# A gated linear-attention block with an NVFP4 feed-forward: two VectorE dequantising instructions of weight chunk 0 moved behind the first attention step's projections and output rows

## The chip, the cores and the metric

The kernel runs on one NeuronCore of one Trainium2 chip. The metric is the device time of one execution in microseconds (us). Core 0 is the only core, so its time is the time of the kernel.

## What is computed

Two residual layers on x of shape 4 x 512 x 512, in float32, each behind a layer norm. The reference, cut to what matters here:

```python
x = x + attn(layernorm(x))      # DIM 512, 4 heads of 128, chunks of 128 tokens
x = x + ffn(layernorm(x))       # MLP_DIM 4096

# attn, per batch row b, head h and chunk n of 128 tokens
q, k, v = x @ Wq + bq, x @ Wk + bk, x @ Wv + bv
k = k / max(norm(k), 1e-12)
alpha, beta = sigmoid(x @ Walpha + balpha), softplus(x @ Wbeta + bbeta)
cla = cumsum(log(alpha + 1e-6))                 # inside the chunk
decay = where(causal, exp(cla - cla.T), 0)
attn = (q @ k.T) * beta.T * decay
y_local = attn @ v
delta = v.T @ (k * beta * exp(cla_end - cla))
y = (q @ state.T) * exp(cla) + y_local
state = state * exp(cla_end) + delta

# ffn: W from two 4-bit codes per byte and one scale per 32 values
gate, up = xt @ Wg.T, xt @ Wu.T
out = (gelu(gate) * up) @ Wd.T
```

## The kernel before, in words

The 2048 tokens are 16 tiles of 128 (`NT = 16`), held in SBUF as `X1`. Every float32 matrix operand of the large products is split into a float16 high part and a float16 low part (what the high part leaves), and three products of parts replace one of float32. The program is written out by hand, engine by engine: TensorE (PE), ScalarE (ACT), VectorE (DVE), GpSimd (POOL) and the SyncE queue (SP) each have their own fixed list of instructions, and semaphores tie the lists together. Nothing is scheduled by a planner, so what stands on an engine's list behind a waiting instruction waits too.

The order of the work is: layer norm and transposes of the 16 tiles with the early q, k, v projections; the gates; then 16 attention steps T = 0 to 15, each one chunk of one batch row; then the feed-forward, whose parts begin inside the attention steps. The change is at the border of attention steps 0 and 1.

What each engine does in a step T, in the order of its list:

- **PE**: `head(T)` transposes the chunk's keys into a PSUM bank, "kn" (L414), and multiplies q by k (L423). Then come the step's fills, which are projections of the next batch rows (L348, twelve matmuls each): in step 0 the keys (1,1) and (1,2), with the decay matrix of step 1 between them; in step 1 the queries (1,2) and the values (1,0). Then `mid(T)`: the state's increment from the weighed keys (L434), the local output from the weighed attention (L440) and, from step 1 on, the global output (L447). In `mid(1)` L434 waits for `weigh_keys(1)` and L440 waits for `weigh(1)`, both on DVE. The PSUM banks are taken in a ring of five (`Banks([0, 1, 5, 6, 7])`); a bank is waited for until the engine that reads it has released it. The bank of "kn" of step 1 is the one that the projection of keys (1,1) filled, so L414 of step 1 waits until DVE has moved that projection to SBUF (L959).
- **ACT**: `norms_of_k(T)` squares and sums the transposed keys (L710), then the exponential of the next step's decay (L700), the fills of kind q (L671), a copy of transposed tokens (L660, from step 1), and, in the steps of `DEQUANTED`, the high part of both halves of a weight chunk (L748). So ACT's list has L748 of chunk 0 ahead of the four L710 of step 1.
- **POOL**: `head(T)` turns the sums into the keys' scales: maximum (L1325), power (L1327), two products (L1329, L1330), then scales the decay (L1333). After that come the mask of the next step (L1316), the decay rows (L1310) and, in the steps of `DEQUANTED`, the low part of both halves of the chunk (L1359). So POOL's list has L1359 of chunk 0 ahead of `head(1)`.
- **DVE**: `weigh_keys(T)` (L1013) needs POOL's L1329; `weigh(T)` (L1023) needs POOL's L1333; the norm of the second layer for the tile before (L932, from step 1); the fills of kinds k (L959) and v (L954); `mid(T)`, which is the state (L1033 or L1040), the output row (L1045, L1052) and the statistics of the new row (L921, L923); the low part of the transposed tokens (L938, from step 1).

A weight chunk k is dequantised in parts. DVE makes the float16 bit patterns from the codes in `dq_bits(k)` (four instructions: L1087, L1093, L1098, L1101) and the float32 weights from bits and scales in `dq_finish(k)` (L1122, one for each of two halves, into the one buffer `wf`). ACT then casts each half to its high part (L748) and POOL subtracts for the low part (L1359). SP may load the chunk after next only when `dq_finish(k)` is done (L1504, L1507).

`DEQUANTED` says in which steps this happens:

```python
DEQUANTED = (0, 1, 4, 5, 8, 9)
```

Chunks 0 to 5 are finished in these steps, and `dq_bits` of each stands at the end of the step before (chunk 0's ahead of step 0). Steps 0 and 1 finish chunks 0 and 1; steps 4 and 5 finish chunks 2 and 3 in the same way.

Of the kernel before, what the change touches and what calls it, by code (L numbers as in the profile page):

```python
# [59 lines left out]
def fills(T):  # L60

    b, c = T // 4, T % 4
    out = [QKV_FIRST[c]] if b == 0 else []
    if b in (1, 2):
        out += [(kind, b + 1, h) for kind, h in KQ[2 * c:2 * c + 2]]
    if T == 0:
        out.insert(0, ("k", 1, 1))
    elif T + 3 < NT:
        out.append(("v", (T + 3) // 4, (T + 3) % 4))
    return out  # L70


DEQUANTED = (0, 1, 4, 5, 8, 9)
# [42 lines left out]
def wlo_count(k, nib):  # L116

    if k < 6:
        return 2 * k + nib + 1
    g, c = k // 6 - 1, k % 6  # L120
    return 12 + 6 * g + {0: 1, 2: 2, 4: 3 + nib, 5: 5 + nib}[c]


def pair_count(k):

    return 2 * (k // 6 - 1) + k % 6 // 2 + 1


def block_kernel(nc, x, wqkv, bqk, bv, wab, bab, codes, scales, out, cla):
    with ExitStack() as ctx:  # L130
# [82 lines left out]
        def h4(ap):  # L213
            return ap.rearrange("p (h t) -> p h t", h=4)
# [24 lines left out]
        def place(k):  # L239
            return k % 2 if k < 10 else 0  # L240
# [7 lines left out]
        def codes_in(k):  # L248

            return tb[:, :] if k < 6 else PS[7 if k < 10 else 5][:, :].bitcast(I32)  # L250
# [661 lines left out]
        def _(eng):  # L912
# [12 lines left out]
            def apply(tag, T):  # L925
                s = T % 2
                dv.wait_ge(s_rstd[tag], 2 * T + 2)
                if T >= 2:
                    dv.wait_ge(s_turn[tag], T - 1)
                elif tag == "n2":  # L930
                    dv.wait_ge(s_turn["n1"], NT - 1 + T)
                eng.tensor_scalar(xh[:, s, :], X1[:, T, :], mv[:, s, 0:1], rs[:, s, 1:2], ALU.subtract,  # L932
                                  ALU.mult).then_inc(s_xh[tag], 1)

            def turn_low(tag, T):
                hi, lo = (XT[:, a, :, 128 * T:128 * T + 128] for a in range(2))
                dv.wait_ge(s_hi[tag], T + 1)
                eng.tensor_tensor(lo, h4(PS[bank_of[tag, T]][:, :]), hi, ALU.subtract).then_inc(s_lo[tag], 1)  # L938
# [8 lines left out]
            def project(kind, b, h):  # L947
                f, done = 1.0 / (XS * QS), 4 * b + h + 1
                if kind == "v":
                    dv.wait_ge(s_const, 64)  # L950
                    dv.wait_ge(s_mm["v"], done)
                    if b >= 1:
                        dv.wait_ge(s_yl, done - 4)
                    eng.scalar_tensor_tensor(vv[:, h, :], PS[bank_of["v", b, h]][:, :], f, bvb[:, :], ALU.mult,  # L954
                                             ALU.add).then_inc(s_qkv["v"], 1)
                elif kind == "k" and b >= 1:
                    dv.wait_ge(s_const, 64)
                    dv.wait_ge(s_mm["k"], done)
                    eng.tensor_scalar(kT[:, b % 2, h, :], PS[bank_of["k", b, h]][:, :], f, bqk_s[:, 4 + h:5 + h],  # L959
                                      ALU.mult, ALU.add).then_inc(s_qkv["k"], 1)  # L960
# [44 lines left out]
            def weigh_keys(T):  # L1005
                b, c, s = T // 4, T % 4, T % 2
                if c < 3:
                    dv.wait_ge(s_kn, T + 1)
                    dv.wait_ge(s_kscale, 4 * T + 3)
                    dv.wait_ge(s_ss, T + 1)  # L1010
                    if T >= 1:
                        dv.wait_ge(s_dl, 3 * b + c)
                    eng.tensor_tensor(h4(kwb[:, :]), h4(PS[bank_of["kn", T]][:, :]),  # L1013
                                      kn_s[:, s, 4, :].unsqueeze(2).broadcast_to([128, 4, 128]),
                                      ALU.mult).then_inc(s_kw, 1)

            def weigh(T):
                s = T % 2
                dv.wait_ge(s_S, T + 1)
                dv.wait_ge(s_decw, T + 1)  # L1020
                if T >= 1:
                    dv.wait_ge(s_yl, T)
                eng.tensor_tensor(att[:, :], PS[4][:, :], dec[:, s, :], ALU.mult).then_inc(s_attn, 1)  # L1023
# [45 lines left out]
            def act_tile(i):  # L1069
                dv.wait_ge(s_gu["up"], i + 1)  # L1070
                inter(i, pair(i)[1][:, :], i + 1)
                inter_low(i)

            def gather(n, tt):
                T = 4 * (n % 4) + tt
                dv.wait_ge(s_dn, 4 * n + tt + 1)
                eng.scalar_tensor_tensor(X1[:, T, :], PS[bank_of["dn", n, tt]][:, :], 1.0 / (WS * IS), X1[:, T, :],  # L1077
                                         ALU.mult, ALU.add).then_inc(s_ev, 1)

            def dq_bits(k):  # L1080
                dq_magnitude(k)
                dq_sign(k)
# [20 lines left out]
            def dq_finish(k):  # L1103
                s, paired = place(k), k >= 6 and k % 6 < 4
                dst = wf2 if paired and k % 2 else wf
                dv.wait_ge(s_dq, 6 * k + 4)
                if paired and k % 2:
                    dv.wait_ge(s_wlo, wlo_count(k - 1, 0))
                    if k == 7:
                        dv.wait_ge(s_turn["n2"], NT)  # L1110
                elif paired:
                    if k % 6 == 2:
                        dv.wait_ge(s_wsum, pair_count(k - 1))
                    else:
                        dv.wait_ge(s_wlo, wlo_count(k - 1, 1))
                for nib in range(2):
                    if not paired and k >= 1:
                        if k >= 6 and k % 6 == 4:
                            dv.wait_ge(s_wsum, pair_count(k - 1))
                        else:  # L1120
                            dv.wait_ge(s_wlo, wlo_count(k - 1, nib))
                    eng.scalar_tensor_tensor(dst[:, nib, :], codes_in(k).bitcast(F16)[:, nib::2], CODE, scl[s],  # L1122
                                             ALU.mult, ALU.mult).then_inc(s_dq, 1)

            def token_sums(b, first=0, last=4):
                dv.wait_ge(s_R, 4 * b + 4)
                steps = ((0, 1, 0), (1, 3, 1), (3, 3, 0), (2, 2, 3))
                for n, (out, x, y) in list(enumerate(steps))[first:last]:
                    if n:
                        dv.wait_ge(s_T, 4 * b + n)  # L1130
                    eng.tensor_tensor(R[b][out], R[b][x], R[b][y], ALU.subtract).then_inc(s_T, 1)
# [47 lines left out]
            dk = 0  # L1179
            for T in range(NT):  # L1180
                i, fill = T - APART, fills(T)
                weigh_keys(T)
                if T == 0:
                    weigh(T)
                if T in DEQUANTED:
                    dq_finish(dk)
                    dk += 1
                if T >= 1:
                    weigh(T)
                if T >= 1:  # L1190
                    apply("n2", T - 1)
                for f in fill:
                    project(*f)
                if T == 10:
                    for tt in range(4):
                        gather(0, tt)
                if i >= 0:
                    act_tile(i)
                    if T >= 14:
                        gather(1, T - 14)  # L1200
                    turn_low("n2", T - 1)
                    mid(T)
                else:
                    mid(T)
                    if T >= 1:
                        turn_low("n2", T - 1)
                if T + 1 in DEQUANTED:
                    dq_bits(dk)
                if T == 13:
                    token_sums(0)  # L1210
# [22 lines left out]
            dk = 10  # L1233
# [359 lines left out]
```

## Time and profile before

| what | value |
|---|---|
| median of 3 runs | 1144.14 us (1143.7 to 1144.48) |
| the profiled execution | 1143.82 us |
| its span, first to last instruction | 1141.8 us |
| PE busy | 1136.0 us, 99% of the span |
| DVE busy | 694.8 us, 61% |
| ACT busy | 446.1 us, 39% |
| POOL busy | 535.3 us, 47% |
| granted TensorE clock, mean | 1.000 |

A row of the timeline gives the start in us from the span's start, the us from the start of the first to the end of the last of the instructions merged in it, the engine, the line of the kernel, the operation, written tile <- read tiles, shape and count; in square brackets stands how long the engine had been idle before it and on which instruction it waited. PE spans overlap, because matmuls are pipelined.

### The profile page before, as it was taken

How to read it: one execution, taken by the hardware profiler on the slowest of the kernel's cores; microseconds unless marked ns; L12 is line 12 of the kernel's file. 1: busy time of each engine (PE TensorE's matmuls, PEld its weight loads, DVE VectorE, ACT ScalarE, POOL GpSimd, SP SyncE). 2: the span in 40 equal slices, each digit the busy share in tenths (PEclk: the TensorE clock that was granted, in tenths of full speed). 3: DMA queues.
4: the chain of work that ended last, by engine and by line, in shares of the span. 5: the costliest groups of instructions: out<-in, count | busy, mean ns of one | idle time of the engine just before them, and what ended most of it. 6: DMA issues, size and time to landing. Idle time of an engine off the chain costs nothing.

```text
span 1141.8 us, 19963 instructions
## 1 busy us (share of the span) xinstructions
PE 1136.0 (99%) x8014; PEld 787.4 (69%) x8014; DVE 694.8 (61%) x1284; ACT 446.1 (39%) x1037; POOL 535.3 (47%) x530
## 2 busy tenths in 40 slices
PE   9999999999999999999999999999999999999999
PEld 5666655565467777777777777777777777777776
DVE  7788656367777855665566556655665566555334
ACT  4433334253344434343434343434343434343332
POOL 3386535155883945363536363635362536253110
PEclk9999999999999999999999999999999999999999
DMA  8021011000101010101010101010101010100111
GB/s 303 3 76 46 29 38 38 10 10 2 56 19 38 20 37 20 38 19 38 20 37 20 38 19 38 20 38 19 38 20 37 18 38 22 34 17 16 38 38 65
DMA packets 22828, 41.97 MB, mean 37 GB/s; under 512 B 2704, under 2 KB 3024, under 8 KB 22736
## 3 DMA queue, kind: packets, MB, share of 16 engines
q1 hardware_dynamic: 22736, 40.70, 11.3%
q8 instruction: 63, 1.03, 0.4%
q14 instruction: 29, 0.24, 0.1%
HBM read 36.46 MB, written 4.23 MB: 36 GB/s over the span
## 4 chain that ended last, share of the span: by engine, by line
PE 96%; POOL 1%; DVE 1%; ACT 0%; issue 0%; DMA 0%; SPq 0%; DVEq 0%; ACTq 0%; POOLq 0%
PE ps L518 45%; PE ps L558 29%; PE ps L348 8%; PE ps L479 7%; PE ps L314 1%; PE ps L440 1%; PE ps L423 1%; PE ps L447 1%; PE ps L434 1%; PE ps L358 1%; PE ps L414 1%; DMA WR<-wqkv 0%; POOL bigA L1302 0%; DVE wf L1122 0%; POOL kn_s L1327 0%
## 5 line engine op out<-in xcount | busy, mean ns | idle before, releaser
L558 PE MATMUL ps<-WR,ihl_s 128*128 128x512 f16 x768 | 184.7, 379 | 0.0
L518 PE MATMUL ps<-XT,WR 128*128 128x256 f16 x1344 | 183.3, 273 | 0.0
L518 PE MATMUL ps<-REG,WR 128*128 128x256 f16 x1344 | 183.3, 273 | 0.0
L1139 DVE TENSOR_TENSOR load<-load,ps 128x256 f32<-128x256 f32 x168 | 70.7, 421 | 179.8 <-PE ps L518 101.3
L558 PE MATMUL ps<-WR,vv 128*128 128x512 f16 x708 | 171.4, 379 | 0.0
L518 PEld LDWEIGHTS ps<-REG,WR 128*128 128x128 f16 x1344 | 131.5, 98 | 39.1
L814 ACT COPY load<-ps 128x256 f32<-128x256 f32 x168 | 62.6, 372 | 245.1 <-PE ps L518 245.1
L1139 DVE TENSOR_TENSOR bigB<-bigB,ps 128x256 f32<-128x256 f32 x168 | 70.6, 420 | 124.3 <-ACT bigB L814 93.2
L518 PEld LDWEIGHTS ps<-XT,WR 128*128 128x128 f16 x1344 | 131.5, 98 | 15.4
L814 ACT COPY bigB<-ps 128x256 f32<-128x256 f32 x168 | 62.6, 373 | 172.0 <-PE ps L518 172.0
L558 PEld LDWEIGHTS ps<-WR,ihl_s 128*128 128x128 f16 x768 | 75.2, 98 | 66.5
L1359 POOL TENSOR_TENSOR WR<-wf,WR 128x512 f16<-128x512 f32 x40 | 48.4, 1229 | 136.6 <-ACT WR L748 136.6
L558 PEld LDWEIGHTS ps<-WR,vv 128*128 128x128 f16 x708 | 69.3, 98 | 59.2
L1343 POOL TENSOR_TENSOR vv<-fw,vv 128x512 f16<-128x512 f32 x54 | 69.4, 1308 | 66.3 <-ACT vv L729 66.3
L1343 POOL TENSOR_TENSOR ihl_s<-fw,ihl_s 128x512 f16<-128x512 f32 x56 | 72.2, 1311 | 57.4 <-ACT ihl_s L729 57.4
L1077 DVE SCALAR_TENSOR_TENSOR X<-ps,X 128x512 f32<-128x512 f32 x127 | 86.6, 682 | 17.4 <-PE ps L558 17.3
L518 PE MATMUL ps<-REG,bigA 128*128 128x256 f16 x672 | 91.7, 273 | 0.0
L348 PE MATMUL ps<-XT,WR 128*128 128x512 f16 x384 | 86.8, 379 | 0.0
L479 PE MATMUL ps<-XT,WR 128*128 128x512 f16 x384 | 85.0, 379 | 0.0
L518 PEld LDWEIGHTS ps<-REG,bigA 128*128 128x128 f16 x672 | 65.8, 98 | 19.6 <-ACT bigB L814 0.2
L1354 POOL TENSOR_TENSOR WR<-bigC,WR 128x512 f16<-128x512 f32 x28 | 34.4, 1248 | 95.2 <-ACT WR L767 95.2
L1061 DVE SCALAR_TENSOR_TENSOR fw<-fw,bigB 128x256 f32<-128x256 f32 x112 | 72.9, 650 | 3.8
(180 smaller groups left out, 1793.6 us busy)
## 6 DMA issues: line engine op xcount, KB each, us to landing
load<-codes SPq DMA_DIRECT2D x48, 256.0 KB
load<-scales SPq DMA_DIRECT2D x48, 256.0 KB
y<-X SPq DMA_DIRECT2D x15, 256.0 KB, 2.0
bigA<-cla SPq DMA_DIRECT2D x14, 256.0 KB, 3.0
X<-x SPq DMA_DIRECT2D x3, 1024.0 KB, 13.2
WR<-wqkv SPq DMA_DIRECT2D x2, 1024.0 KB, 9.6
X<-x SPq DMA_DIRECT2D x4, 256.0 KB, 3.9
WR<-wqkv SPq DMA_DIRECT2D x4, 256.0 KB, 4.3
```

Of the source, the lines that this page charges most:

```text
L314: t = eng.transpose(PS[bank][:, 128 * kt:128 * kt + 128], src, ident[:, :])
L348: mm = eng.matmul(PS[bank][:, :], lhs, rhs, start=(n == 0), stop=(n == 11))
L479: mm = eng.matmul(bank[:, :], buf[:, wp, o + kt, 128 * j:128 * j + 128], XT[:, xp, kt, 512 * b:512 * b + 512], start=(n == 0), stop=(n == 11))
L518: mm = eng.matmul(half_bank(kind, name), w(wp, kt), x(xp, kt), start=(first and n == 0), stop=(n == 5), skip_group_check=True)
L558: mm = eng.matmul(PS[bank][:, :], ih[:, ip, 128 * tt:128 * tt + 128], buf[:, wp, 8 + j, :], start=(j == 0 and p == 0), stop=(j == end and ...
L814: eng.copy(start, half_bank(kind, name)).then_inc(s_snap, 1)
L1061: eng.scalar_tensor_tensor(w, w, GS * IS, pu, ALU.mult, ALU.mult).then_inc(s_inter, 1)
L1077: eng.scalar_tensor_tensor(X1[:, T, :], PS[bank_of["dn", n, tt]][:, :], 1.0 / (WS * IS), X1[:, T, :], ALU.mult, ALU.add).then_inc(s_ev, 1)
L1139: eng.tensor_tensor(c, c, half_bank(kind, end), ALU.add).then_inc(s_comb, 1)
L1343: eng.tensor_tensor(ih[:, 1, :], fw[:, i % 2, :], ih[:, 0, :], ALU.subtract).then_inc(s_ilop, 1)
L1354: eng.tensor_tensor(buf[:, 1, base + nib, :], wf2[:, nib, :], buf[:, 0, base + nib, :], ALU.subtract).then_inc(s_wl1, 1)
L1359: eng.tensor_tensor(buf[:, 1, base + nib, :], wf[:, nib, :], buf[:, 0, base + nib, :], ALU.subtract).then_inc(s_wlo, 1)
```

## The change

```diff
@@ -1180,13 +1180,10 @@
             for T in range(NT):
                 i, fill = T - APART, fills(T)
                 weigh_keys(T)
-                if T == 0:
-                    weigh(T)
-                if T in DEQUANTED:
+                if T in DEQUANTED and T > 0:
                     dq_finish(dk)
                     dk += 1
-                if T >= 1:
-                    weigh(T)
+                weigh(T)
                 if T >= 1:
                     apply("n2", T - 1)
                 for f in fill:
@@ -1204,6 +1201,9 @@
                     mid(T)
                     if T >= 1:
                         turn_low("n2", T - 1)
+                if T == 0:
+                    dq_finish(dk)
+                    dk += 1
                 if T + 1 in DEQUANTED:
                     dq_bits(dk)
                 if T == 13:
```

Only DVE's list differs, and only in step 0: `dq_finish(0)`, two instructions, stands behind `mid(0)` and no longer ahead of the two projections. Steps 1 and later, and all the other engines' lists, are as they were.

DVE's list at the end of step 0, as a difference between the kernel before and the change (REG is the key buffer, ps a PSUM bank, bigA the state, X the token tile, bst and mv its statistics, wf the chunk's float32 weights, load and tb its codes and bits):

```order
 L1013 TENSOR_TENSOR bigB<-ps,kn_s 128x512
 L1023 TENSOR_TENSOR bigB<-ps,bigB 128x512
-L1122 SCALAR_TENSOR_TENSOR wf<-tb,load 128x512 x2
 L959 TENSOR_SCALAR REG<-ps,bqk_s 128x512 x2
 L1033 COPY bigA<-ps 128x512
```
```order
 L921 BN_STATS bst<-X 128x6
 L923 BN_AGGR mv<-bst 128x2
+L1122 SCALAR_TENSOR_TENSOR wf<-tb,load 128x512 x2
 L1087 SCALAR_TENSOR_TENSOR load<-load 128x512
 L1093 TENSOR_SCALAR tb<-load 128x512
```

L1122 has moved behind six instructions of step 0 and stands directly ahead of `dq_bits(1)`.

POOL's list from the end of step 0 into step 1, the same in both kernels, with the semaphores that each row waits for (WR is the weight buffer, kn_s the keys' scales, bigB decay and attention):

```order
L1310 TENSOR_TENSOR bigA<-bigA,bigD 128x512 [waits s_cla,s_rows0]
L1359 TENSOR_TENSOR WR<-wf,WR 128x512 [waits s_whi] x2
L1325 TENSOR_SCALAR kn_s<-kn_s 128x4 [waits s_ss]
L1327 TENSOR_TENSOR kn_s<-kn_s,half 128x4 [waits s_kscale]
L1329 TENSOR_TENSOR kn_s<-kn_s,bigD 128x4 [waits s_kscale]
L1330 TENSOR_TENSOR kn_s<-kn_s,bigD 128x4
L1333 TENSOR_TENSOR bigB<-bigB,kn_s 128x512 [waits s_kscale,s_mask]
```

Nothing moved here: L1359 of chunk 0, which needs ACT's cast and so DVE's L1122, stands ahead of step 1's five instructions for the keys' scales.

## Rows read from the trace of the kernel before

**Rows 1.** The page, section 1, busy us and share of the span
```profile
PE 1136.0 (99%) x8014; PEld 787.4 (69%) x8014; DVE 694.8 (61%) x1284; ACT 446.1 (39%) x1037; POOL 535.3 (47%) x530
```

**Rows 2.** Chain that ended last, at the end of step 0: start, us, what
```profile
65.49 1.95 DVE wf L1122 x2
67.44 0.67 DVE REG L959
```

**Rows 3.** Timeline of PE, end of step 0 and step 1
```profile
62.87 2.75 PE L348 MATMUL ps<-XT,WR 128*128 128x512 f16 x12
...
66.35 1.06 PE L440 MATMUL ps<-vv,bigB 128*128 128x128 f32 x8
68.16 0.66 PE L414 MATMUL ps<-bigC,REG 128*128 128x128 f32 x4 [0.75 <-DVE REG L959]
...
74.72 1.05 PE L434 MATMUL ps<-vv,bigB 128*128 128x128 f32 x8
75.79 1.13 PE L440 MATMUL ps<-vv,bigB 128*128 128x128 f32 x8
```

**Rows 4.** Timeline of DVE, end of step 0 and step 1
```profile
65.41 2.03 DVE L1122 SCALAR_TENSOR_TENSOR wf<-tb,load 128x512 f32<-128x512 f16 x2
67.36 1.40 DVE L959 TENSOR_SCALAR REG<-ps,bqk_s 128x512 f32<-128x512 f32 x2
...
69.28 0.67 DVE L1045 TENSOR_TENSOR X<-X,ps 128x512 f32<-128x512 f32 x1
...
70.81 0.66 DVE L1087 SCALAR_TENSOR_TENSOR load<-load 128x512 int32<-128x512 int32 x1
...
72.91 0.68 DVE L1013 TENSOR_TENSOR bigB<-ps,kn_s 128x512 f32<-128x512 f32 x1
...
74.97 0.68 DVE L1023 TENSOR_TENSOR bigB<-ps,bigB 128x512 f32<-128x512 f32 x1
```

**Rows 5.** Timeline of ACT, chunk 0's casts and step 1's first square
```profile
66.87 1.22 ACT L748 CAST WR<-wf 128x512 f16<-128x512 f32 x2 [3.21 <-DVE wf L1122]
68.85 0.28 ACT L710 ACTIVATE bigD<-ps 128x128 bf16<-128x128 f32 x1 [0.76 <-PE ps L414]
```

**Rows 6.** Timeline of POOL, chunk 0's low parts and step 1's scales
```profile
67.57 2.28 POOL L1359 TENSOR_TENSOR WR<-wf,WR 128x512 f16<-128x512 f32 x2 [1.28 <-ACT WR L748]
...
71.52 0.48 POOL L1329 TENSOR_TENSOR kn_s<-kn_s,bigD 128x4 f32<-128x4 f32 x1
```

**Rows 7.** The line view of L1122, 60 to 130 us: ns min/median/max
```profile
L1122 DVE SCALAR_TENSOR_TENSOR wf<-tb,load x8: 677/801/1432, 65.4 to 116.6; 128x512 f32<-128x512 f16 x8
```

**Rows 8.** Timeline of ACT, POOL and DVE, end of step 4 and step 5
```profile
108.91 1.14 ACT L748 CAST WR<-wf 128x512 f16<-128x512 f32 x2
109.61 2.72 POOL L1359 TENSOR_TENSOR WR<-wf,WR 128x512 f16<-128x512 f32 x2 [3.89 <-ACT WR L748]
110.08 1.23 DVE L1087 SCALAR_TENSOR_TENSOR load<-load 128x512 int32<-128x512 int32 x1
111.34 1.27 DVE L1093 TENSOR_SCALAR tb<-load 128x512 int32<-128x512 int32 x1
...
114.93 0.69 DVE L1013 TENSOR_TENSOR bigB<-ps,kn_s 128x512 f32<-128x512 f32 x1 [1.26 <-POOL kn_s L1329]
...
117.25 0.68 DVE L1023 TENSOR_TENSOR bigB<-ps,bigB 128x512 f32<-128x512 f32 x1
```

**Rows 9.** Timeline of ACT and DVE, end of step 1 and step 2
```profile
78.80 1.14 ACT L748 CAST WR<-wf 128x512 f16<-128x512 f32 x2
...
83.58 0.69 DVE L1013 TENSOR_TENSOR bigB<-ps,kn_s 128x512 f32<-128x512 f32 x1 [2.33 <-POOL kn_s L1329]
```

**Rows 10.** SP's load of chunk 2, and DVE's first use of it
```profile
67.47 0.33 SPq L1504 DMA_DIRECT2D load<-codes  x1
...
99.23 0.68 DVE L1087 SCALAR_TENSOR_TENSOR load<-load 128x512 int32<-128x512 int32 x1
```

**Rows 11.** Windows: us, busy of PE, PEld, DVE, ACT, POOL, then PEclk
```profile
66.00:70.00 4.00, 3.25 (x28) 2.81 (x27) 3.97 (x7) 2.37 (x11) 2.57 (x3) 1.00 0.38 101
```

## The prediction

> **What bounds the kernel.** I read the page's busy line first. PE is busy 1136.0 us of a span of 1141.8 us [rows 1], so a change of the time has to come from PE's few idle moments, or from new ones. Then I read the chain that ended last, for the places where it leaves PE. At the end of step 0 it does: it runs through both L1122 of `dq_finish(0)`, then through one L959, and only then back to PE [rows 2]. PE's own timeline shows the same gap: L440 of step 0 ends at 66.35 + 1.06 = 67.41, and L414 of step 1 starts at 68.16 after 0.75 us idle, released by L959 [rows 3]. DVE ran L959 only after 2.03 us of L1122 [rows 4]. That 0.75 us is what the change can win, and it is the whole of it: from 68.16 on PE runs without a gap worth naming up to L434 at 74.72 and L440 at 75.79 [rows 3].
>
> The next question is what stands close behind. L440 of step 1 starts 0.82 us after DVE's L1023 (75.79 - 74.97) [rows 3, 4], and L1023 takes 0.68 us, so PE was already released by DVE at the last moment. Whatever makes `weigh(1)` late makes PE late by the same amount.
>
> **What the change moves.** On DVE both L1122 go behind two L959, L1033, L1045, L921 and L923. No instruction is added or removed.
>
> *The projections.* The first L959 starts at 65.41, where L1122 did. The second needs the matmuls that end at 62.87 + 2.75 = 65.62 [rows 3] and follows it. L414 of step 1 then waits for nothing: **-0.75 us**, if nothing later takes it back.
>
> *The output row.* L1045 waits for L440 of step 0, which ends at 67.41, and starts at about 67.44. From the start of L1045 to the start of what follows L923 it was 70.81 - 69.28 = 1.53 us [rows 4]. So the first L1122 starts at 67.44 + 1.53 = 68.97, 3.56 us later than before. Before, it took up to 1.43 us beside GpSimd's work; undisturbed it takes 0.68 us [rows 7], and POOL has nothing to do here, since its list stands at L1359. It ends at 69.65 and ACT's first cast starts at 69.68, against 66.87 [rows 5]: 2.81 us late.
>
> *What is queued behind it.* This is what decides. ACT's list has the two casts ahead of step 1's four L710; POOL's has the two L1359 ahead of step 1's scales. Before, the casts lay in a hole (ACT then still waited 0.76 us for L414 [rows 5]) and L1359 ended at 69.85, before the squares were done [rows 6]. Now casts, squares, L1359, L1325, L1327, L1329 are one chain to DVE's L1013, and then L1333 and L1023 follow, and PE's L440 waits at the end. DVE has `dq_finish(1)` between L1013 and L1023, as before.
>
> *How long that chain is.* The trace of before has a twin of it: at steps 4 and 5 the two L1359 of chunk 2 run beside `dq_bits(3)` and ahead of step 5's scales. There it is 114.93 - 108.91 = 6.02 us from the first cast to L1013 and 117.25 - 108.91 = **8.34 us** to L1023 [rows 8]. There the bit instructions and L1359 hinder one another: L1087 takes 1.23 us, against 0.66 us in step 0 [rows 4], and the L1359 pair 2.72 us, against 2.28 us [rows 6]. The lower bound is step 2, where L1359 of chunk 1 runs with no bit instruction beside it: 83.58 - 78.80 = 4.78 us to L1013 [rows 9]; with the 74.97 - 72.91 = 2.06 us from L1013 to L1023 of step 1 [rows 4] that is 6.84 us.
>
> I take the twin, because the change puts `dq_bits(1)` directly behind L1122: L1087 would start at about 70.2, and L1359 wants to start 0.70 us after the cast, at 70.4. The two then overlap as at 110.08, with the same instructions on both sides. The rule in the Trainium skill's page "SBUF — State Buffer" (section "Who interferes with whom") says that a VectorE instruction with two SBUF inputs and a GpSimd instruction that reads SBUF exclude each other for whole instructions, whoever comes second waiting. By that rule the quiet interval doesn't apply here and the sum is that of the twin; without the rule it would be the quiet one, 1.55 us below. The 1.23 us of L1087 agree with it.
>
> *The sum.* L1023 of step 1 starts at 69.68 + 8.34 = 78.02, PE's L440 at 78.02 + 0.82 = 78.84, against 75.79: **+3.05 us**. The quiet chain gives 69.68 + 6.84 + 0.82 = 77.34: +1.55 us. The 0.75 us won at L414 is not subtracted: it only makes PE arrive at L434 sooner, at 73.97, and wait there for L1013, which starts at 69.68 + 6.02 = 75.70 (before: 72.91), and then again at L440.
>
> *What comes after.* From L1023 of step 1 on, DVE's list runs on as before and so does PE's; both are late by the same 3 us, and everything later, ACT and POOL too, is released by them. PE then has no idle time in which to catch up. SP's load of chunk 2 waits for both L1122, so it leaves about 3 us later than 67.47; its first use is at 99.23 [rows 10], so it costs nothing. The decay row that follows on SP's list moves with it and has a step to spare.
>
> Against the profiled execution of 1143.82 us this is 1146.9; the median of the runs is 1144.14, 0.3 us above that execution, so the forecast is **1147.1 us**.
>
> **The rivals.** 0.2% of the time is 2.29 us; smaller differences can't be told from no change here, so the border is at 1146.43 us.
>
> *A: the twin's chain, +3 us.* As above, 1147.1 us; from +2.3 to +3.8 us if the instructions interlock differently.
>
> *B: the quiet chain, not slower by the border.* L1087 comes just ahead of L1359 instead of just behind it, and `dq_bits(1)` may be through sooner. The place is POOL between L1359 and L1329. The price is +1.55 us, 1145.7 us. It decides if L1023 starts less than 7.58 us after the first cast (2.29 us late at PE); the twin has 8.34 us and the quiet steps 6.84 us. For it speaks that only a part of the 1.5 us has to go; against it, that L1359 is 2.3 us long and all four bit instructions fall beside it.
>
> *C: the won 0.75 us stays.* PE would go straight through, 1143.4 us, if L1023 of step 1 started by 74.97 - 0.75 = 74.22. That is 4.54 us after the cast, less than the 4.78 us that even L1013 needs in the quiet case. Nothing in the rows allows it, and its 0.07% would still count as no change.
>
> *D: the clock falls.* PE is idle for most of the time from 73.97 to 78.84, with only L434's 1.05 us in it. With 0.75 us idle in the window from 66 to 70 us the granted clock stayed at 1.00 (2.4 GHz) [rows 11]; no row shows so long a pause. At 1.2 GHz a group of twelve matmuls would take about 2.75 us more [rows 3]; two such groups make +8.5 us in all, 1152.6 us. The Trainium skill's page "TensorE: Matmul & The Clock Gate" (Part 1) says that idleness brings the lower clock; no row here shows it fall.
>
> **The numbers.** A 0.75, B 0.19, C 0.02, D 0.04. The time is A's. The range goes from B's quiet end with the spread of the runs, 1145.5, to A with 0.8 us more of interlocking and the same spread, 1148.1; it leaves out C and D and the rims of A and B. Slower by over 0.2% is A nearly whole and D: 0.78. Within 0.2% is B, C and A's rim: 0.21. Faster by over 0.2%: 0.01, since the largest gain in sight is 0.75 us.
>
> **What would show it.** In the changed kernel's timeline: L414 of step 1 at about 67.4 without a wait for L959; the first L1122 near 69.0, at 0.68 us; the first cast at 69.7; L1087 or L1359 clearly longer than 0.66 and 1.16 us; L1013 of step 1 at 75 to 76 with an idle DVE ahead of it, released by L1329; PE idle ahead of L434 and L440, the latter starting near 78.8; and then every row later by one and the same amount. It is wrong if L440 starts before 78.08 (B), if the delay shrinks in later steps, or if ACT's squares of step 1 come before its casts.

## The result, and the profile after

| | before | changed |
|---|---|---|
| median | 1144.07 us (6 runs, 1143.7 to 1144.48) | 1148.57 us (6 runs, 1147.15 to 1149.18) |
| ratio | | 1.0036, 95% interval 1.0023 to 1.0049 |
| profiled execution | 1143.82 us, span 1141.8 | 1147.18 us, span 1145.2 |

The change makes the kernel slower, by 4.5 us in the median (the two medians alone would give a ratio of 1.0039). About 3 us had been forecast, and the range ended at 1148.1 us: the measured time lies outside it. The six executions don't scatter as those of before do. Two took 1147.15 and 1147.18 us, both with a mean granted clock of 1.000; the other four took 1148.48 to 1149.18 us, all with a mean clock below 1.000 (0.999, 0.999, 0.999, 0.997). The profiled execution is one of the two, so I first read in it the part that the forecast was about, and come to the clock with the experiments.

PE's timeline of the changed kernel, end of step 0 and step 1, against [rows 3]:

```profile
66.96 1.06 PE L440 MATMUL ps<-vv,bigB 128*128 128x128 f32 x8
67.86 0.60 PE L414 MATMUL ps<-bigC,REG 128*128 128x128 f32 x4
...
76.90 1.13 PE L434 MATMUL ps<-vv,bigB 128*128 128x128 f32 x8 [2.37 <-DVE bigB L1013]
...
79.20 1.13 PE L440 MATMUL ps<-vv,bigB 128*128 128x128 f32 x8 [1.17 <-DVE bigB L1023]
```

The wait at L414 is gone. In its place PE waits 2.37 us for L1013 and 1.17 us for L1023. L440 of step 1 starts at 79.20 instead of 75.79, 3.41 us later, and the span has grown by the same 3.4 us. Not all of that belongs to the change. The chain's first long piece is the load of the first weights, here and before:

```profile
2.16 4.80 DMA WR<-wqkv
```

It was 4.19 us in the profiled execution of before, 0.61 us less, and L440 of step 0 is late by exactly this (66.96 against 66.35 in [rows 3]), long before anything has changed. What is left, 3.41 - 0.61 = **2.80 us**, arises between there and L440 of step 1. In the same way I take out of every later profile how late its L440 of step 0 starts against the 66.35 of [rows 3]; over all the profiles that is 0.15 to 0.87 us.

The same stretch on DVE, ACT and POOL, against [rows 4 to 6]:

```profile
68.06 0.69 DVE L1045 TENSOR_TENSOR X<-X,ps 128x512 f32<-128x512 f32 x1
...
69.61 1.26 DVE L1122 SCALAR_TENSOR_TENSOR wf<-tb,load 128x512 f32<-128x512 f16 x2
70.30 1.22 ACT L748 CAST WR<-wf 128x512 f16<-128x512 f32 x2 [6.02 <-DVE wf L1122]
70.78 0.68 DVE L1087 SCALAR_TENSOR_TENSOR load<-load 128x512 int32<-128x512 int32 x1
...
70.99 2.78 POOL L1359 TENSOR_TENSOR WR<-wf,WR 128x512 f16<-128x512 f32 x2 [4.09 <-ACT WR L748]
...
71.42 0.27 ACT L710 ACTIVATE bigD<-ps 128x128 bf16<-128x128 f32 x1
71.50 1.26 DVE L1093 TENSOR_SCALAR tb<-load 128x512 int32<-128x512 int32 x1
...
72.68 1.38 DVE L1098 TENSOR_SCALAR load<-load 128x512 int32<-128x512 int32 x1
...
75.77 0.20 POOL L1329 TENSOR_TENSOR kn_s<-kn_s,bigD 128x4 f32<-128x4 f32 x1
...
76.06 0.69 DVE L1013 TENSOR_TENSOR bigB<-ps,kn_s 128x512 f32<-128x512 f32 x1 [1.27 <-POOL kn_s L1329]
...
78.37 0.68 DVE L1023 TENSOR_TENSOR bigB<-ps,bigB 128x512 f32<-128x512 f32 x1
```

The chain is the one of the forecast: cast, L1359 beside the bit instructions, scales, L1013, L1023. The first cast starts at 70.30, which is 69.69 without the start's 0.61 us; 69.68 had been forecast. From there it is 5.76 us to L1013 and 8.07 us to L1023. One thing differs from the twin in steps 4 and 5: there L1359 began before L1087 (109.61 and 110.08 in [rows 8]), here L1087 begins first, 0.21 us ahead, and takes its quiet 0.68 us.

### The profile page after: what moved, and what is told of

It is laid out like the page before. It is cut to its first block, busy times and chain, and to the rows that moved or that the text cites. A ratio compares the mean times of both kernels' runs of the same rounds, so it can differ in the third digit from the quotient of the medians.

```text
span 1145.2 us, 19963 instructions
## 1 busy us (share of the span) xinstructions
PE 1135.9 (99%) x8014; PEld 787.0 (69%) x8014; DVE 696.2 (61%) x1284; ACT 445.5 (39%) x1037; POOL 535.1 (47%) x530
## 4 chain that ended last, share of the span: by engine, by line
PE 96%; DVE 1%; POOL 1%; DMA 0%; ACT 0%; issue 0%; SPq 0%; DVEq 0%; ACTq 0%
PE ps L518 45%; PE ps L558 29%; PE ps L348 9%; PE ps L479 7%; PE ps L314 1%; PE ps L440 1%; PE ps L423 1%; PE ps L447 1%; PE ps L434 1%; PE ps L358 1%; PE ps L414 1%; POOL WR L1359 0%; DMA WR<-wqkv 0%; DVE wf L1122 0%; POOL kn_s L1327 0%
## 5 line engine op out<-in xcount | busy, mean ns | idle before, releaser
L1359 POOL TENSOR_TENSOR WR<-wf,WR 128x512 f16<-128x512 f32 x40 | 48.8, 1240 | 139.5 <-ACT WR L748 139.5
L348 PE MATMUL ps<-XT,WR 128*128 128x512 f16 x384 | 86.8, 379 | 0.0
```

The source lines that it names most:

```text
L348: mm = eng.matmul(PS[bank][:, :], lhs, rhs, start=(n == 0), stop=(n == 11))
L1359: eng.tensor_tensor(buf[:, 1, base + nib, :], wf[:, nib, :], buf[:, 0, base + nib, :], ALU.subtract).then_inc(s_wlo, 1)
```

## The experiments

I had two theories after this reading. One, the chain: 2.8 us of PE waiting, because chunk 0's parts now stand ahead of step 1's squares and scales on ACT and POOL while they are late. Two, the clock: PE's pause sometimes costs clock as well, and that is what lifts the median from 1147.1 to 1148.6 us. The rival to the second was that six executions are few and scatter.

### The changed kernel once more (label again)

Edit: none.

> The changed kernel, unchanged, once more. Theory (chain and clock): its time is the time before plus about 2.8 us of PE waiting at L434 and L440 of step 1, and in part of the executions 1.3 to 2 us more, each of those with a mean granted clock below 1.000; so single executions lie in two groups, near 1147.1 and near 1148.7 us. Rival (the six earlier executions were scatter of the start's loads, 0.6 us in the profiled one): one group with a spread like that of before, some 0.8 us, and no tie between time and clock.

Measured: 1148.82 us median of 5 (1148.14 to 1149.5), ratio 1.0040 (1.0027 to 1.0053); before, on the same chip, 1144.11 us. All five have a mean clock below 1.000; two of them, 1148.82 and 1149.5 us, have 0.997. With the first six that is 9 of 11 executions with a lowered clock, and not one of the 65 executions of before that ran beside the experiments has it. This time the profiled execution is such a one. Its windows (us, busy of PE, PEld, DVE, ACT, POOL with the number of instructions, then PEclk, the DMA share and GB/s):

```profile
70.00:74.00 4.00, 4.00 (x21) 1.77 (x19) 3.96 (x5) 3.36 (x12) 2.75 (x2) 1.00 0.33 104
74.00:78.00 4.00, 1.62 (x9) 1.04 (x8) 2.70 (x4) 0.00 (x0) 3.61 (x7) 0.92 0.26 92
78.00:82.00 4.00, 3.54 (x22) 3.28 (x22) 4.00 (x10) 0.00 (x0) 2.83 (x4) 0.65 0.44 116
82.00:86.00 4.00, 4.00 (x29) 2.81 (x28) 2.81 (x8) 3.19 (x12) 2.18 (x2) 1.00 0.06 15
```

and PE in it:

```profile
77.16 1.85 PE L434 MATMUL ps<-vv,bigB 128*128 128x128 f32 x8 [2.38 <-DVE bigB L1013]
...
79.46 1.77 PE L440 MATMUL ps<-vv,bigB 128*128 128x128 f32 x8 [0.46 <-DVE bigB L1023]
81.07 1.06 PE L447 MATMUL ps<-bigA,REG 128*128 128x128 f32 x8
```

The granted clock leaves 1.00 (2.4 GHz) behind PE's wait for L1013 and is back before 82; from 78 to 79 alone it is 0.50, that is 1.2 GHz. In the profiled execution with the full clock L434 and L440 took 1.13 us each; here they take 1.85 and 1.77 us, 64 and 57% more. L434's part is hidden, because PE waits for L1023 anyway and only waits less (0.46 us instead of 1.17). L440's part is not: it costs 0.64 us. This is the fastest of the five executions, and where a dip falls otherwise it can cost more, as two profiles below show (1.7 us each).

### PE kept busy in both waits (label warm_pause)

```diff
                     dl = bank_of["dl", T] = banks.take(pe, (s_state, 3 * b + c + 1))
+                    if T == 1:
+                        for _ in range(18):
+                            eng.transpose(PS[dl][:, 0:128], ident[:, :], ident[:, :])
...
                 yl = bank_of["yl", T] = banks.take(pe, (s_yla, T + 1))
+                if T == 1:
+                    for _ in range(9):
+                        eng.transpose(PS[yl][:, 0:128], ident[:, :], ident[:, :])
```

> The changed kernel with PE kept busy in its two waits of step 1 by 27 dummy transposes: 18 ahead of L434, 9 ahead of L440 (about 0.11 us each, so 2.0 and 1.0 us in waits of 2.4 and 1.2 us). Clock theory: the clock stays at 1.000 in every execution, and all lie near 1147.1 us, in one group; the chain on ACT, POOL and DVE is as it was, so the profile still shows L440 of step 1 about 2.8 us late. Rival (the lower clock has nothing to do with the pause of PE): the slower group stays, 1148.5 us and over in about half of the executions.

Measured: 1146.73 us median of 10 (1146.5 to 1147.7), ratio 1.0025 (1.0015 to 1.0034), all ten with a clock of 1.000. PE's waits are 0.31 and 0.16 us instead of 2.37 and 1.17:

```profile
73.94 2.13 PE L434 MATMUL ps<-bigC 128*128 128x128 f32 x18
76.39 1.16 PE L437 MATMUL ps<-vv,bigB 128*128 128x128 f32 x8 [0.31 <-DVE bigB L1019]
77.38 1.15 PE L443 MATMUL ps<-bigC 128*128 128x128 f32 x9
78.69 1.16 PE L446 MATMUL ps<-vv,bigB 128*128 128x128 f32 x8 [0.16 <-DVE bigB L1029]
```

(Lines have moved by the added ones: L437 and L446 are L434 and L440 of the other kernels.) PE's product for the local output starts at 78.69, 2.90 us later than the 75.79 of before [rows 3]. Of this 0.19 us is the start's (L440 of step 0 is at 66.54), so the chain still costs 2.7 us. From the first cast it is 5.76 us to L1013, as in the changed kernel. The lowered clock is gone in every execution. So it was the idle PE that brought it. Against the run `again`, which ran beside this one, the median is 2.1 us lower; against the first six executions it is 1.8 us.

### Only the first wait filled (label warm_first)

Edit: as above, without the nine transposes ahead of L440.

> The changed kernel with only the 18 dummy transposes ahead of L434, none ahead of L440. Clock theory, first pause decides: clock 1.000 in all, near 1146.9 us as with both. Rival, the whole idle time near step 1 decides or the second pause alone is enough: 1.2 us idle is left and part of the executions shows a clock below 1.000 and 1.3 us and more above the others.

Measured: 1147.0 us median of 9 (1146.51 to 1147.25), all with a clock of 1.000:

```profile
76.48 1.16 PE L437 MATMUL ps<-vv,bigB 128*128 128x128 f32 x8 [0.31 <-DVE bigB L1016]
78.88 1.13 PE L443 MATMUL ps<-vv,bigB 128*128 128x128 f32 x8 [1.23 <-DVE bigB L1026]
```

A wait of 1.23 us for `weigh(1)` (L1023, here L1026), with 0.31 us ahead of it, is left in this kernel and doesn't bring the clock down.

### A pause of PE without the change (label pause_alone)

On the kernel before, L1013 of step 1 is repeated:

```diff
+                    for r in range(4 if T == 1 else 0):
+                        eng.tensor_tensor(h4(kwb[:, :]), h4(PS[bank_of["kn", T]][:, :]),
+                                          kn_s[:, s, 4, :].unsqueeze(2).broadcast_to([128, 4, 128]),
+                                          ALU.mult).then_inc(s_pad, 1)
+                        dv.wait_ge(s_pad, r + 1)
                     eng.tensor_tensor(h4(kwb[:, :]), h4(PS[bank_of["kn", T]][:, :]),
```

> The kernel before (no instruction moved), with L1013 of step 1 repeated four times on DVE, about 0.72 us each, ahead of the one that PE waits for. Clock theory: a pause of PE of some 2.9 us at the same place is enough: 1147.0 us in part of the executions, 1148.3 to 1149 us with a mean clock below 1.000 in the others. Rival (the slower group comes from something else in the changed order, such as later loads): all near 1147.0 us with a clock of 1.000.

Measured: 1146.83 us median of 10. Seven executions at a clock of 1.000 took 1146.41 to 1147.33 us; the three at 0.999 took 1147.55, 1148.02 and 1148.11 us. All three lie under the 1148.3 to 1149 us expected of this group. PE waits here 0.75 us at L414, and then:

```profile
76.83 1.13 PE L434 MATMUL ps<-vv,bigB 128*128 128x128 f32 x8 [1.76 <-DVE bigB L1018]
...
78.63 1.13 PE L440 MATMUL ps<-vv,bigB 128*128 128x128 f32 x8 [0.67 <-DVE bigB L1028]
```

So a pause of PE at this place brings the lowered clock in a kernel in which no instruction was moved. It does so more rarely, 3 in 10 against 9 in 11, with shorter waits.

### Chunk 1's bit instructions made small (label small_bits)

```diff
+                cut = slice(0, 16 if k == 1 else 512)
-                eng.scalar_tensor_tensor(raw[s], raw[s], 12, raw[s], ALU.logical_shift_left,
+                eng.scalar_tensor_tensor(raw[s][:, cut], raw[s][:, cut], 12, raw[s][:, cut], ALU.logical_shift_left,
```

and the same cut in the other three.

> The changed kernel with the four bit instructions of chunk 1 on 16 columns instead of 512 (the other 496 columns of chunk 1 are left unmade, so less is computed). Collision theory: with the bit instructions gone from beside L1359, it is 4.8 us from ACT's first cast to L1013 of step 1 (5.76 us in the changed kernel) and about 6.9 us to L1023 (8.07 us); L440 of step 1 is 1.6 us late instead of 2.8, 1145.7 us, and PE's pause is so much shorter that the clock stays at 1.000. Rival (the list order alone makes the delay, the collisions nothing): 5.8 and 8.1 us as before, 1147.1 us or more.

Measured in the profile, ACT, POOL, DVE and PE:

```profile
70.18 1.22 ACT L748 CAST WR<-wf 128x512 f16<-128x512 f32 x2 [6.02 <-DVE wf L1125]
...
70.87 2.29 POOL L1362 TENSOR_TENSOR WR<-wf,WR 128x512 f16<-128x512 f32 x2 [4.09 <-ACT WR L748]
...
74.86 0.69 DVE L1013 TENSOR_TENSOR bigB<-ps,kn_s 128x512 f32<-128x512 f32 x1 [1.66 <-POOL kn_s L1332]
...
75.69 1.13 PE L434 MATMUL ps<-vv,bigB 128*128 128x128 f32 x8 [1.29 <-DVE bigB L1013]
...
77.17 0.68 DVE L1023 TENSOR_TENSOR bigB<-ps,bigB 128x512 f32<-128x512 f32 x1
...
78.00 1.95 PE L440 MATMUL ps<-vv,bigB 128*128 128x128 f32 x8 [1.18 <-DVE bigB L1023]
79.73 1.91 PE L447 MATMUL ps<-bigA,REG 128*128 128x128 f32 x8
```

4.68 us from the first cast to L1013 (74.86 - 70.18) and 6.99 us to L1023, against 5.76 and 8.07 us with the bit instructions at full size. The pair on POOL (L1359, here L1362) takes 2.29 us, its quiet time of [rows 6], instead of 2.78. L440 is 2.21 us later than before, 1.72 us of it without the start's 0.49 (L440 of step 0 is at 66.84). So 1.08 us of the 2.8 is the collision of `dq_bits(1)` with POOL's work, and the remaining 1.7 us is the order of the lists.

The second half of the expectation failed. The clock did not stay: six of eight executions show 0.999 or 0.997, and the median is 1147.14 us, not 1145.7. Only the fastest, 1145.65 us at 1.000, is where the shorter chain alone would put it; the other one at 1.000 took 1146.33 us. The profiled execution, with a clock of 0.999, shows the price of a dip with nothing to hide it: L440 takes 1.95 us and L447 1.91 us, against 1.13 and 1.06 us in the profiled execution of the changed kernel, together 1.7 us lost.

### Only behind the projections (label between)

```diff
                 for f in fill:
                     project(*f)
+                if T == 0:
+                    dq_finish(dk)
+                    dk += 1
...
-                if T == 0:
-                    dq_finish(dk)
-                    dk += 1
                 if T + 1 in DEQUANTED:
```

> The two instructions put only half as far back: behind the two projections, ahead of the output row. Chain theory: L414 of step 1 no longer waits (0.75 us less), ACT's first cast comes near 67.6 us, so squares and scales of step 1 are not behind it, and L1013 and L1023 of step 1 start when DVE's own list gets to them, as before (about 72.9 and 75.0 us); L440 starts near 75.8, so the 0.75 us is lost again there and the time is that of before, 1144.1 us, with a clock of 1.000. Rival (any move of the chunk's parts behind the projections costs): 1145 us or more.

Measured: 1144.06 us median of 11, ratio 1.0001 (0.9992 to 1.0010), clock 1.000 in all. ACT's casts start at 67.58, ahead of its squares, which start at 68.71, no later than before (68.85 in [rows 5]). On PE:

```profile
67.39 0.60 PE L414 MATMUL ps<-bigC,REG 128*128 128x128 f32 x4
...
73.90 1.05 PE L434 MATMUL ps<-vv,bigB 128*128 128x128 f32 x8
75.97 1.13 PE L440 MATMUL ps<-vv,bigB 128*128 128x128 f32 x8 [1.02 <-DVE bigB L1023]
```

The wait at L414 has turned into one of 1.02 us for L1023: nothing is won, as expected: L440 starts at 75.97, and without the start's 0.15 us that is 75.82, against 75.79 before. But for 0.21 us ahead of L1013, DVE is busy without a break from L959 of step 0 to L1023 of step 1, and `dq_finish(1)` is ahead of L1023. 1.02 us of idle PE left the clock at 1.000 in all eleven executions.

### Chunk 1's two behind L1023 as well (label weigh_first)

Edit: as in the run `between`, and in step 1 `dq_finish(1)` behind `weigh(1)`.

> As the run with the two instructions behind the projections, and chunk 1's two instructions also put behind L1023 of step 1. Chain theory: L1023 now waits only for POOL's L1333, near 74.0 us, so PE has no wait in step 1, keeps the 0.75 us, and the time is 1143.4 us, clock 1.000. Rival (the later parts of chunk 1 hold up step 2 as those of chunk 0 held up step 1): 1144 us or more, with L434 or L440 of step 2 waiting.

Measured: 1144.4 us median of 11, ratio 1.0002 (0.9993 to 1.0010), clock 1.000. That is the rival's number (1144 us or more), but not at the rival's place. L440 starts at 75.23 without a wait, so the chain to it is right. But PE then waits at the next place:

```profile
75.23 1.13 PE L440 MATMUL ps<-vv,bigB 128*128 128x128 f32 x8
76.19 1.06 PE L447 MATMUL ps<-bigA,REG 128*128 128x128 f32 x8
77.96 0.74 PE L314 MATMUL ps<-bigC,bigA 128*128 128x128 f32 x4 [0.71 <-DVE bigA L932]
```

L932, the norm of the row before, stood behind the two L1122 and itself took 1.26 us instead of 0.77. It was not the late parts in step 2, but DVE's own list again. I had asked only who waits for L1023.

### Chunk 0's parts behind step 1's squares and scales on ACT and POOL (label own_queue)

Against the changed kernel: ACT and POOL, each with the same edit (POOL's stands behind `head(T)`), and DVE:

```diff
                 norms_of_k(T)
+                if T == 1:
+                    dequant(dk)
+                    dk += 1
...
-                if T in DEQUANTED:
+                if T in DEQUANTED and T > 0:
                     dequant(dk)
                     dk += 1
...
-                if T in DEQUANTED and T > 0:
+                if T in DEQUANTED and T > 1:
                     dq_finish(dk)
                     dk += 1
                 weigh(T)
+                if T == 1:
+                    dq_finish(dk)
+                    dk += 1
```

> The changed kernel (chunk 0's two instructions behind the output row), but on ACT and POOL the parts of chunk 0 stand behind step 1's squares and scales, and on DVE chunk 1's two instructions behind L1023 of step 1. Theory (the lists of ACT and POOL carry the delay): step 1's squares start near 68.3 us, L1023 by 74 us, no pause of PE before L440, 1143.4 to 1144.2 us, clock 1.000. Rival (the late L1122 itself costs, by DVE's list or its collisions): L440 stays 1 us or more late, 1145 us or more.

Measured: 1147.4 us median of 7 (1146.98 to 1148.02), a mean clock below 1.000 in all seven. The time is a miss; the place, L440, is a hit. PE, and DVE's `dq_finish(1)` (here L1125):

```profile
75.19 1.06 PE L440 MATMUL ps<-vv,bigB 128*128 128x128 f32 x8
76.08 1.06 PE L447 MATMUL ps<-bigA,REG 128*128 128x128 f32 x8
79.82 0.74 PE L314 MATMUL ps<-bigC,bigA 128*128 128x128 f32 x4 [2.69 <-DVE bigA L935]
80.42 0.91 PE L414 MATMUL ps<-bigC,REG 128*128 128x128 f32 x4
81.13 1.91 PE L423 MATMUL ps<-REG 128*128 128x128 f32 x8
82.84 3.38 PE L348 MATMUL ps<-XT,WR 128*128 128x512 f16 x12
...
75.98 2.61 DVE L1125 SCALAR_TENSOR_TENSOR wf<-tb,load 128x512 f32<-128x512 f16 x2 [1.34 <-POOL WR L1365]
```

ACT's squares of step 1 start at 68.42, and L440 doesn't wait at all, with chunk 0's L1122 as late as in the changed kernel. L1013 starts at 72.87, ahead of `dq_finish(1)` in either list, so the wait at L434 was made by the order of ACT's and POOL's lists. At L440 this run changes two things at once, since chunk 1's L1122 no longer stand ahead of L1023 either. An estimate: with the 2.31 us from L1013 to L1023 of the changed kernel and 0.8 us to PE, L440 would start at 76.0, or 75.5 without the start's 0.54 us, no later than the 75.79 of before. So their lists account for the lost time at L440 as well, though PE would still wait a little there. And `wf` is one buffer: `dq_finish(1)` must wait until POOL has read chunk 0 out of it, DVE stands idle 1.34 us for that, and L932 (here L935) is behind it. PE's pause has only moved to L314, a single one of 2.69 us, and it brings the lowered clock every time. The dip costs 1.7 us here, by L414, L423 and L348 against their 0.66, 1.06 and 2.75 us of before.

### Both chunks behind the projections of their steps (label both_later)

Against the changed kernel:

```diff
-                if T in DEQUANTED and T > 0:
+                if T in DEQUANTED and T > 1:
...
                 for f in fill:
                     project(*f)
+                if T in (0, 1):
+                    dq_finish(dk)
+                    dk += 1
...
-                if T == 0:
-                    dq_finish(dk)
-                    dk += 1
```

> Chunk 0's two instructions behind the projections of step 0, chunk 1's two behind the projections of step 1 (so behind L1023, L932 and L954). Chain theory: the 0.75 us at L414 is won, L440 goes straight through, and L932 is no longer behind chunk 1's parts, so L314 doesn't wait either: 1143.4 us, 0.7 us under the time before, which five rounds can just tell, and no PE wait in the profile of step 1. Rival (the late chunk 1 holds up ACT's and POOL's step 2 and with it L434 or L440 there): 1144 us or more.

Measured: 1143.29 us median of 11 (1142.89 to 1143.63); before, beside it, 1144.2 us of 15 (1143.79 to 1144.7). The ratio is 0.9992; its interval, 0.9983 to 1.0001, touches 1, but the two sets of times don't overlap. In step 1 PE has almost no wait left:

```profile
75.08 1.13 PE L440 MATMUL ps<-vv,bigB 128*128 128x128 f32 x8
76.05 1.06 PE L447 MATMUL ps<-bigA,REG 128*128 128x128 f32 x8
76.94 0.64 PE L314 MATMUL ps<-bigC,bigA 128*128 128x128 f32 x4
...
79.08 2.76 PE L348 MATMUL ps<-XT,WR 128*128 128x512 f16 x12 [0.17 <-DVE bigA L1040]
```

This is the 0.75 us of L414, kept: L440 starts 0.91 us earlier than the 75.79 of before, without the start's 0.20 us, and a wait of 0.17 us for L1040 takes some of it back. It is under what the forecast called measurable (0.2%).

## Why the prediction was wrong

- **The direction, the bound and the gain at L414**: right. The kernel is slower by over 0.2%, and the wait of 0.75 us is gone without showing in the time.
- **The first cast**: 69.68 forecast, 69.69 measured without the start's 0.61 us. L1122 ran at its undisturbed time, since POOL had nothing to do.
- **The chain from cast to L1023**: 8.34 us forecast from the twin in steps 4 and 5, 8.07 us measured; 6.84 us was the quiet bound, and with the collision removed 6.99 us was measured. The term +3.05 us measured 2.80 us. (The quiet chain is 1.50 us below the twin, not 1.55 us as the forecast has it once.) The interval of the twin came out well, but not for the reason given. The forecast's own starts, 70.2 for L1087 and 70.4 for L1359, have them in the other order than the twin, which is rival B's condition, and so it came: L1087 ran ahead and took its quiet 0.68 us. The instructions behind it were held up instead: L1093 and L1098 take 1.26 and 1.38 us beside the pair on POOL, against 0.43 and 0.42 us in step 0 of before, and the pair takes 2.78 us. That the order hardly mattered was not foreseen; so far the agreement is luck. The rule in the Trainium skill's page "SBUF — State Buffer" (section "Who interferes with whom"), as the forecast gives it, is about instructions with two SBUF inputs, and L1093 and L1098 read one tile; the same section also lists `tensor_scalar`, in its two-port modes, among those that can contend with GpSimd, and the trace agrees as far as the times go. No run shows the mode.
- **What comes after**: right, the delay stays as it is to the end. The two executions at the full clock took 1147.15 and 1147.18 us where 1147.1 was forecast, but 0.61 us of the profiled one is its start, which the forecast didn't have. The fairer test is the two kernels with the waits filled, 1146.73 and 1147.0 us.
- **Rival D, the clock**: this is the step that failed. The forecast left the clock out of its sum and its range and gave it 4 in 100, because the clock had stayed at 1.00 through 0.75 us of idle time [rows 11], and no row showed so long a pause. That row says nothing of two waits of 2.4 and 1.2 us. It happened in 9 of 11 executions. Its price was wrong too: 5.5 us beyond A, for two groups of twelve matmuls at half the clock. Three profiles show 0.6 us (the changed kernel again), 1.7 us (small bits) and 1.7 us (own queue); in the first six executions those with a lowered clock lie 1.3 to 2.0 us above the other two, and filling PE's waits lowered the median by 1.6 to 2.1 us. A's 1147.1 us and some 1.5 us of this make up the measured 1148.57 us, but that price is taken from the result; it isn't a forecast. The Trainium skill's page "TensorE: Matmul & The Clock Gate" (Part 1) says that idleness brings the lower clock. The run with the waits filled (1.000 in ten of ten) and the one with a pause alone (3 of 10 lowered) agree.
- **Rivals B and C**: the quiet chain didn't come; its length was confirmed. C's claim that nothing in the rows lets L1023 start by 74.22 held for this change. With `dq_finish(1)` left where it was (the run `between`) nothing was won; with it moved as well (`both_later`) it is worth 0.9 us by the medians, with an interval that touches no change.

One thing stays open. What decides in which executions the clock falls was not found: waits of 1.29 and 1.18 us brought it down in 6 of 8, and 0.75, 1.76 and 0.67 us, no less in sum, in 3 of 10. I can say only that it never fell with a single wait of up to 1.23 us (20 executions of two kernels, one of them with 0.31 us ahead of it), and always with one of 2.69 us (7).

## What to carry to other kernels

An instruction moved later on one engine drags its consumers along, and what matters is what stands behind them in the lists of the other engines: here two casts on ACT and two subtractions on POOL held up the next step's scales and cost 2.8 us where 0.75 us was to be won. Look for a twin of the new order elsewhere in the trace and take its interval whole; it holds the collisions, too; but check that the instructions meet in the same order. And when a sum leaves TensorE waiting twice within a few us, as here (2.4 and 1.2 us, or 1.3 and 1.2), in a kernel that otherwise keeps it busy, count a lowered clock as a likely case, at a price of 0.6 to 2 us as measured here, and look at single executions, not at one profile: the profiled one here was of the minority.

## What the runs showed of the hardware that I had not expected

The granted clock fell after PE's waits of 2.4 and 1.2 us in 9 of 11 executions of one program, after 1.3 and 1.2 us in 6 of 8, and after a single one of 2.7 us in all seven; where a profile caught it, it was back within 4 us. Filling the longer wait with 18 dummy transposes, which compute nothing, made the kernel 1.6 us faster in the median (1147.0 against 1148.57 us). And bit instructions of 16 columns, of which the first two took 0.17 us each while POOL's pair was only beginning, still stand for a whole instruction of POOL when they come beside it:

```profile
70.95 1.14 DVE L1100 TENSOR_SCALAR load<-load 128x16 int32<-128x16 int32 x1
...
72.12 1.08 DVE L1103 TENSOR_TENSOR tb<-tb,load 128x16 int32<-128x16 int32 x1
```

POOL is held up as well, but there the loss shrinks with the size: POOL's pair lost 0.50 us to instructions of 512 columns and nothing to those of 16.
